# Value matmuls ahead of the second FFN matmul in the second slot of a step: a six-layer local-attention kernel

## The reference, cut to what matters

```python
qkv = shift_tokens(x) @ Wqkv                    # 16 heads of 64
q, k = l2norm(q) * q_scale, l2norm(k) * k_scale
q, k = rotary(q), rotary(k)
sim  = q @ k_of_own_and_previous_window.T * 8   # windows of 32 tokens
x    = softmax(mask(sim)) @ v @ Wo + x          # attention, with the residual
t    = layernorm(shift_tokens(x)) @ W1 + b1     # 128 -> 2 x 341
a, gate = split(t)
x    = (a * gelu(gate)) @ W2 + b2 + x           # 341 -> 128: "the second FFN matmul"
```

## Time and profile before

| | |
|---|---|
| median of 3 runs | 1732.7 us |
| lowest and highest | 1731.18 and 1740.07 us |
| profiled execution, first to last instruction (span) | 1731.0 us; no other time of its own is recorded |
| TensorE matmul busy | 1639.0 us, 95% |
| VectorE, ScalarE, GpSimd busy | 84%, 82%, 76% |
| time of a step in the steady part | 33.63 us |
| mean granted TensorE clock | 0.986 |

### The profile page before, as it was taken

How to read it: one execution, slowest core, us unless ns; L and a number is a source line. 1 busy time by engine, 2 the same in 40 slices (tenths; PEclk the granted TensorE clock), 3 DMA queues, 4 the chain that set the end, 5 groups by cost and what they waited for, 6 DMA issues and landing times.

```text
span 1731.0 us, 68758 instructions
## 1 busy us (share of the span) xinstructions
PE 1639.0 (95%) x25970; PEld 1277.2 (74%) x25970; DVE 1446.3 (84%) x3011; ACT 1425.6 (82%) x2851; POOL 1311.9 (76%) x1305
## 2 busy tenths in 40 slices
PE   7779999999999999999999999999999999999995
PEld 5657777777777777777777777777777777777773
DVE  4499888888888888888888888888888888888884
ACT  3367888888888888888888888888888888888885
POOL 6088877877877787787778778787877877777765
PEclk9799999999999999999999999999999999999997
DMA  4111111111111111111111111111111101111000
GB/s 140 41 38 43 35 33 36 30 48 38 41 32 30 36 36 42 49 30 32 30 36 42 49 36 30 32 30 48 38 41 36 30 27 38 35 30 32 28 24 26
DMA packets 41426, 66.40 MB, mean 38 GB/s; under 512 B 7072, under 2 KB 16032, under 8 KB 41376
## 3 DMA queue, kind: packets, MB, share of 16 engines
q1 hardware_dynamic: 40224, 65.38, 12.7%
q10 hardware_dynamic: 1152, 0.34, 0.1%
HBM read 20.61 MB, written 1.05 MB: 13 GB/s over the span
## 4 chain that ended last, share of the span: by engine, by line
PE 61%; ACT 28%; issue 6%; DVE 4%; ACTq 1%; DMA 0%; POOL 0%; DVEq 0%; POOLq 0%
PE ps_qs L530 12%; PE ps_po L530 9%; PE ps_q L530 8%; PE ps_a L530 7%; PE ps_tk L530 7%; PE ps_f L530 6%; PE ps_po L650 5%; ACT p_bd L943 4%; PE ps_k L530 4%; PE ps_v L530 4%; ACT squares L949 4%; ACT L1053 3%; ACT L1050 3%; ACT q_t L943 3%; ACT prob L987 2%
## 5 line engine op out<-in xcount | busy, mean ns | idle before, releaser
L427 POOL TENSOR_TENSOR qk<-qk,rnorm 128x512 f32<-128x512 f32 x384 | 393.6, 1046 | 176.6 <-DVE rnorm L1284 176.1
L419 POOL TENSOR_TENSOR qk<-qk,qk_rot 128x512 f32<-128x512 f32 x384 | 483.8, 1282 | 0.0
L434 POOL TENSOR_TENSOR prob<-prob,row_inv 128x512 f32<-128x512 f32 x192 | 200.7, 1045 | 92.8 <-DVE row_inv L1301 92.8
L1289 DVE TENSOR_REDUCE row_max<-ps_qs 128x8 f32<-128x512 f32 x191 | 132.0, 691 | 164.8 <-PE ps_qs L530 164.8
L943 ACT COPY p_bd<-ps_po 64x512 f32<-64x512 f32 x378 | 219.1, 580 | 58.8 <-PE ps_po L650 56.4
L1264 DVE TENSOR_REDUCE ssq<-squares 128x8 f32<-128x512 f32 x384 | 261.4, 681 | 3.4 <-ACT squares L949 3.4
L530 PEld LDWEIGHTS ps_qs<-k_t,q_t 64*32 64x32 f32 x12224 | 179.2, 107 | 69.0 <-issue 68.9
L943 ACT COPY attn_t<-ps_po 128x512 f32<-128x512 f32 x191 | 112.5, 589 | 133.2 <-PE ps_po L530 133.1
L530 PE MATMUL ps_qs<-k_t,q_t 64*32 64x64 f32 x12224 | 210.1, 218 | 0.0
L530 PE MATMUL ps_po<-p_bd,v_back 128*64 128x64 f32 x3056 | 193.2, 225 | 0.0
L530 PEld LDWEIGHTS ps_po<-p_bd,v_back 128*64 128x64 f32 x3056 | 163.1, 137 | 35.8 <-issue 17.0
(11 more groups left out here) (237 smaller groups left out, 4082.7 us busy)
## 6 DMA issues: line engine op xcount, KB each, us to landing
v_back<-v_own SPq DMA_DIRECT2D x192, 192.0 KB, 2.4
w_raw<-in_wqkv SPq DMA_DIRECT2D x48, 192.0 KB, 2.4
v_back<-v_own SPq DMA_DIRECT2D x96, 64.0 KB, 2.1
wo_sb<-in_wo SPq DMA_DIRECT2D x12, 256.0 KB, 2.9
w_sb<-in_w SPq DMA_DIRECT2D x6, 341.0 KB, 3.1
w_sb<-in_w SPq DMA_DIRECT2D x6, 192.0 KB, 2.7
x_in<-in_x SPq DMA_DIRECT2D x4, 256.0 KB, 4.2
out<-s_out SPq DMA_DIRECT2D x8, 128.0 KB, 1.9
```

The lines of the kernel that those rows point to most:

```text
L419: nc.gpsimd.tensor_tensor(qk[:, s, i, :], qk[:, s, i, :], qk_rot[:, s, i, :], ALU.add).then_inc(added, 1)
L427: nc.gpsimd.tensor_tensor(heads(qk[:, s, i, :]), heads(qk[:, s, i, :]), rnorm[:, s, 8 * i:8 * i + 8].unsqueeze(2).to_broadcast([P, 8, HEAD ...
L434: nc.gpsimd.tensor_tensor(heads(prob[:, s, :]), heads(prob[:, s, :]), row_inv[:, s, :].unsqueeze(2).to_broadcast([P, 8, HEAD]), ALU.mult). ...
L1289: V.tensor_reduce(row_max[:, s, :], heads(ps[:]), AX, ALU.max).then_inc(max_done, 1)
```

## The change

In slot 1 (j == 1), TensorE issues `values` of unit u-4 in front of `ff_down` of batch n-4 instead of behind it. No instruction is added or removed on any engine, and no semaphore, buffer or bank changes. `drain()` stays as it was.

```diff
@@ -804,8 +804,6 @@
                             ln_mean(n - 2)
                         if live_batch(n - 3):
                             ff_up(n - 3, 0)
-                        if live_batch(n - 4):
-                            ff_down(u - 2, n - 4)
                     if j == 2:
                         if live_batch(n - 2):
                             ln_variance(n - 2)
@@ -818,6 +816,8 @@
                             out_projection(n - 1, 0)
                     if live(u - 4):
                         values(u - 4, n - 1, j, j % 2)
+                    if j == 1 and live_batch(n - 4):
+                        ff_down(u - 2, n - 4)
 
             def drain():
                 a, b, c, d = END - 4, END - 3, END - 2, END - 1
```

## The result

| | before | after |
|---|---|---|
| median, us | 1732.3 (4 runs, 1731.2 to 1740.1) | 1690.7 (4 runs, 1689.9 to 1691.2) |
| profiled span, us | 1731.0 | 1688.4 |
| a step in the steady part, us | 33.63 | 32.71 |
| wait for the copied keys | 44 times, 38.2 us | none |

The account below looks back on a forecast made before the run. TensorE bounds the kernel, waiting 0.87 us a step for ScalarE's copied keys. Terms 1.04 + 0.99 + 1.41 = 3.44 us against 4.28 gain 0.84 us, 37.0 over 44 steps: 1732.7 to 1695.7 us, range 1689.0 to 1702.8.

Parts of the forecast that it names:

- The last term: Slot 1, start of the second FFN matmul to slot 2's first projection: 1.41 us, with bounds of 1.30 and 1.62.
- All that was costed at nothing: Values' own waits, ScalarE's attention copy, later second FFN matmul end, VectorE's and GpSimd's shortened idling: no cost to the step.
- the first term: Slot 1, start of the FFN's first matmul to start of the moved values: 1.04 us, read from slot 2.
- the second term: Slot 1, start of the values to start of the second FFN matmul: 0.99 us, read from the drain.
- the gain without a drain at the change of shape: FFN's first matmul to values: without the drain there, 0.09 us a step more gain, 41.0 us in all.
- the margin: Second FFN matmul in slot 1: reached at 813.50, 0.14 us after the copied keys would let it go at 813.36.
- rival 1: More gain, down to ScalarE's floor: 1.09 us a step, 1684.7 us; with the shape change, 0.99 us, 1689.1. Chance 0.10.
- The rule on shapes: Changing TensorE's tiling mode drains it; 0.09 us after the FFN's first matmul, 0.10 before the projection; changes stay two.
- Rival 2: Slot 1's keys wait partly back: ScalarE 0.4 us later gives 0.26 us a step, 11.4 us, 1707.1 us. Chance 0.07.
- Rivals 3 and 4: 3: GpSimd and VectorE take the gain back, 1732.7 us, chance 0.02. 4: late VectorE read before softmax, 1759.1, chance 0.01.

## Why the prediction was right or wrong

**Right.** The bound and its cause: a wait of 0.87 us in each of 44 steps, set by ScalarE, gone after the move. The last term, second FFN matmul to projection, which no row showed: 1.41 us taken, 1.41 measured. Values to second FFN matmul: 0.99 taken from the drain, 0.98 measured. All that was costed at nothing cost nothing; VectorE kept 0.50 us of idling before slot 2's softmax where I had worked out 0.60. In slot 3 the time from its subtraction to TensorE's turning of q shrank from 0.34 to 0.32 us, because its Newton step already met GpSimd's split, and that was still cover enough. The clock stayed at 1.00.

**Wrong: the first term.** "FFN's first matmul to values: this pair stands next to each other in slot 2, 1.04 us." The pair is the same but its predecessor is not. Slot 2's FFN piece stands behind one-column matmuls and is 1.11 us long; slot 1's stands behind the mean and is 1.03 us long. Both lengths were in my rows. Taking the modelled end less the same 0.07 us of overlap would have given 1.03 - 0.07 = 0.96, which is what was measured. The run with the variance later shows the cause: the same piece in slot 2 is 1.03 us long once the one-column matmuls no longer stand in front. With the 0.01 of the second term this is 0.09 us a step, 4 us: 37.0 forecast, 41.0 found. The prediction also names 41.0 us, as the gain without a drain at the change of shape. That this is the figure found is chance: the drain's 0.09 us are still paid (0.96 us to the values, 0.87 to a follower of the same shape), and the 0.09 us came from the shorter piece. The other 1.8 us between the two spans are the start of the program, which no step of mine covered and which differs from run to run.

**Wrong: the margin, and what a reported wait is worth.** I gave 0.14 us to the keys; it was 0.04 to 0.05, since TensorE arrives 0.09 us earlier than I had it. The range's lower end was rival 1's floor of 0.99 us a step, 43.6 us. The steps stayed above it (0.93 us), so they alone do not leave the range: 1732.7 - 41.0 = 1691.7 us. It took the 4 us of the mis-sized term together with the start, of which the range took no account, and with the spread of a few runs.

**The rule on shapes.** The Trainium skill ("TensorEngine Tiling (Array Packing)", Key Properties) says that a change of tiling mode drains TensorE. The runs agree, with the number beside it: two changes are worth 0.35 us here, in both directions. My 0.09 and 0.10 us per change were the visible gap alone. They made no error in the sum, since the number of changes stayed the same.

**The rivals.** Rival 2 (the wait comes back) is real but needed another edit: it appears when ScalarE's keys are 0.65 us later, and, nearly unseen, when slot 0 gets shorter. Rivals 3 and 4 did not occur. VectorE is indeed next, but in slot 3, only after 0.35 us more are taken off TensorE, and only where GpSimd's split holds it. One reading of the prediction was wrong without harm: it puts the other engines' largest waits on TensorE, but GpSimd's is on VectorE (`rnorm`, 176.1 us), and nothing in the sum rested on that.

## What to carry to other kernels

Work that is ready, put in front of a wait, is worth the whole wait and the lost overlap around it, provided that the path that ends the wait starts earlier than the moved work; compare the two paths from their common start. Take the cost of a pair of operations from a place where the one before the pair is the same too. After such a change look at the new margin: here a further edit that shortened TensorE by 0.35 us brought nothing until ScalarE's path was shortened too, and then VectorE took half of it. An engine that arrives earlier can also meet another one at a new point: look for small instructions that have become long.

## What the runs showed of the hardware

- A wait of TensorE that the profile reports is shorter than what it costs, by the overlap of the modelled end before it with the next start: 0.87 us reported for 0.93 (overlap 0.07 behind the FFN's first matmul), 0.43 for 0.60 (0.17 behind the values). Waits of 0.19 and 0.31 us were not reported at all; 0.12 and 0.14 us of them were left by the same count. Starts against a kernel without the wait show them.
- From the end of a ScalarE copy to the start of the TensorE matmul that waits for it there are 0.19 us (0.18 to 0.20 in 42 of 44 steps), in the kernel before and in four of the experiments.
- Two changes between 128-column and 64-column matmuls cost 0.35 us of TensorE, 0.10 us each as a gap and the rest in longer first instructions behind it.
- Matmuls of one output column make the FFN piece behind them 0.08 us longer.
- A VectorE instruction on 128 x 18 numbers that starts beside GpSimd's weight split ends 0.02 to 0.05 us after it, in all 36 steps of each of eight profiled kernels: 0.17 us long without such a meeting, up to 0.85 with it. In a ninth kernel, where it starts in the last 0.1 us of the split, it keeps its 0.17 us.
- The time at which the first steps begin varies by 5.6 us between profiles (124.6 to 130.2 us), and by 3.7 us between two profiles of the same kernel (126.40 and 130.10); differences of a few us are better read from the steps.
